# Centred output weights and regrouped output steps in a fused linear-attention and expert kernel

## The chip, the cores and the metric

One core of a Trainium2 chip runs the whole kernel in one launch. The metric is the device time in microseconds of that core, from the first to the last instruction of a launch.

## The reference

```python
x = hidden_states                                  # (2, 4096, 256)
x = x + layernorm(attn(layernorm(x)))
x = x + layernorm(ffn(layernorm(x)))

# attn: 8 heads of 32; causal, no softmax, chunks of 64, a running state
q, k, v = h @ Wq.T, h @ Wk.T, h @ Wv.T
inter  = qq @ state                                # per chunk
intra  = (qq @ kk.T * tril) @ vv
state  = state + kk.T @ vv
o = (inter + intra) / max(|sum(q * cumsum(k))|, 1)
o = rmsnorm(o) * norm_w
out = o @ Wo.T

# ffn: 8 experts, I = 256, soft routing weights w(x)
out = sum_e w_e * ((silu(h @ Wg[e]) * (h @ Wu[e])) @ Wd[e])
```

The layer norms have no weights, and eps is 1e-5.

## The kernel before

Each of the 16 blocks takes 256 rows of both batches (512 tokens, four tiles of 128). While the feed-forward part of block i-1 runs expert by expert, the attention of block i is done piece by piece between the experts' steps. An fp32 product is three products of rounded parts (high x high, low x high, high x low), so each operand has a `_hi` copy that ScalarE makes and a `_lo` remainder that VectorE makes. PE does all products in `products` (line 436).

**The order of the work** is written out by hand. `STEPS` has 28 entries; each engine walks through them in `rest` and `first_expert`. In `rest`, for expert e and half m, PE does `up(e, m)`, entry `4e-4+2m`, `down(e-1, m)`, entry `4e-3+2m`. VectorE does `hidden(e, m)` (line 1002), the first entry, `add_down(e-1, m)` (line 1024), `low_hidden(e, m)` (line 899), the second entry; ScalarE does `silu`, entry, `high`, entry. An engine does its own share of each step, in the order of its queue, and waits on semaphores for the others. GpSimd does entries 4 to 27 in a row, and of these only the carry of the state and the inverse square roots (an add and a power, lines 1193 and 1194 in `root_only`, or four instructions, lines 1184 to 1187, in `inverse_root`). The first block has its own lists, `FIRST_PE`, `FIRST_ACT`, `FIRST_DVE` and `FIRST_POOL`, with small matmuls (`warm`) between PE's steps.

**The steps the change touches**, p being a half of the block's tokens:

- `ot`: PE transposes the normalised attention output, ScalarE copies it, VectorE makes its remainder. `wo`: PE multiplies by the output weights; ScalarE copies the result from PSUM to `rows`.
- `ln2_stats`: VectorE takes bn_stats and bn_aggr of `rows` and subtracts the mean in place (line 977). `ln2_add`: x1 = rows * rstd + xs (line 985). `ln3_stats`: statistics of x1. `ln3_apply`: ScalarE normalises x1 into `rows` (line 711) with GpSimd's `rstd` and `shift`. `ft`: PE transposes it (line 591); half p waits for half p of `x1n_ready`. `ft_out`: ScalarE and VectorE make `ft_hi` and `ft_lo`, which the next block's experts read.
- `su`: VectorE adds the two chunk products of a half to the running state, eight additions on 32 partitions each (line 949).
- The PSUM tensor `att_ps` has two halves used in turn: step number n waits until step n-2 has been read out (`READ_OUT`).
- At the start, VectorE scales the rows of the output weights by `norm_w` (line 1137), ScalarE rounds them, VectorE makes the remainder, and SyncE loads the 24 expert units through eight staging buffers as these come free (`stage_free`, line 415).
- At the end, each half of the last block gets statistics, `inverse_root` on GpSimd, normalisation on ScalarE (line 711) and an addition on VectorE (line 381), and is stored.

## Time and profile before

| | us |
|---|---|
| median of 3 runs | 1494.8 (1493.81 to 1496.97) |
| the profiled execution | 1496.2, span 1494.5 |
| PE busy | 1465.5 (98%) |
| VectorE busy | 1023.8 (69%) |
| ScalarE busy | 647.2 (43%) |
| GpSimd busy | 442.9 (30%) |
| mean granted TensorE clock | 0.995 of full speed |

The span is the time from the first to the last instruction of the profiled execution, and the rest of its time lies around it. The page has the busy time of each engine, the span in 40 slices and the costliest groups of instructions. Matmuls are pipelined and their ends are modelled, so that gaps of PE are better read from start to start. Blocks 2 to 14 repeat each other to 0.1 us, with a period of 90.12 us (`ft` at 779.38 and 869.50).

### The profile page before, as it was taken

Reading aid. Unit: us, or ns where it says so; the run is one execution under the profiler, and the core shown is the slowest. Engines: PE = TensorE matmul, PEld = TensorE weight load, DVE = VectorE, ACT = ScalarE, POOL = GpSimd, SP = SyncE. Lnnn points to the kernel's source line nnn. Section 1 sums busy time; section 2 is a strip of 40 time slices with the busy share of each in tenths; the row PEclk is TensorE's granted clock in tenths of the full one; section 3 lists DMA queues with packets and bytes.
Section 4 is the critical chain, followed back from the end, with each engine's and each line's share of the span. In section 5 each row is a group of like instructions: output and inputs, shape, how many; then the busy total and the mean of one; then the engine's idle time right before and its main releaser. Section 6 shows DMA issues by size and latency. Waiting matters only on the chain. (4 is left out here: it accounts for less than half of the span.)

```text
span 1494.5 us, 37390 instructions
## 1 busy us (share of the span) xinstructions
PE 1465.5 (98%) x14438; PEld 1279.1 (86%) x14438; DVE 1023.8 (69%) x2492; ACT 647.2 (43%) x1189; POOL 442.9 (30%) x653
## 2 busy tenths in 40 slices
PE   7799999999999999999999999999999999999997
PEld 6688888888888888888888888888888888888886
DVE  6667667676776767667675776767667676776765
ACT  5443534445354443534445354443534445344333
POOL 1403414133251233414134141232413234141231
PEclk9899999999999999999999999999999999999999
DMA  5100000000000000000000000000000000000000
GB/s 171 57 2 15 15 0 14 14 14 14 0 18 10 14 14 9 19 0 14 14 14 14 0 14 14 14 14 0 28 0 14 14 14 14 0 14 16 2 8 22
DMA packets 25345, 24.59 MB, mean 16 GB/s; under 512 B 2016, under 2 KB 25056, under 8 KB 25312
## 3 DMA queue, kind: packets, MB, share of 16 engines
q1 hardware_dynamic: 25312, 24.13, 5.1%
q8 instruction: 23, 0.38, 0.1%
q14 instruction: 10, 0.08, 0.0%
HBM read 15.74 MB, written 8.39 MB: 16 GB/s over the span
## 5 line engine op out<-in xcount | busy, mean ns | idle before, releaser
L1002 DVE TENSOR_TENSOR late<-late,up_ps 128x512 f32<-128x512 f32 x256 | 174.9, 683 | 155.7 <-PE up_ps L436 99.1
L705 ACT ACTIVATE h_hi<-late 128x512 fp32r<-128x512 f32 x256 | 161.6, 631 | 247.2 <-DVE late L1002 247.2
L436 PE MATMUL down_ps<-w_hi,h_hi 128*128 128x256 f32 x976 | 264.5, 293 | 0.0
L786 ACT ACTIVATE late<-gate_ps 128x512 f32<-128x512 f32 x256 | 152.3, 595 | 252.1 <-PE gate_ps L436 252.1
L436 PE MATMUL down_ps<-w_hi,h_lo 128*128 128x256 f32 x976 | 254.1, 282 | 0.0
L1225 POOL TENSOR_TENSOR rms_in<-rms_in,minus_half 128x16 f32<-128x16 f32 x32 | 93.4, 2919 | 498.3 <-DVE rms_in L958 498.3
L899 DVE TENSOR_TENSOR h_lo<-late,h_hi 128x512 fp32r<-128x512 f32 x256 | 175.7, 686 | 65.0 <-ACT h_hi L705 65.0
L1024 DVE SCALAR_TENSOR_TENSOR late<-down_ps,route,late 128x256 f32<-128x256 f32 x364 | 158.4, 477 | 87.9 <-PE down_ps L436 84.9
L436 PE MATMUL gate_ps<-ft_hi,w_hi 128*128 128x512 f32 x512 | 204.9, 400 | 1.0 <-ACT ft_hi L705 0.8
L436 PE MATMUL gate_ps<-ft_hi,w_lo 128*128 128x512 f32 x512 | 203.5, 397 | 0.0
L436 PE MATMUL up_ps<-ft_hi,w_hi 128*128 128x512 f32 x512 | 199.7, 390 | 0.0
L436 PE MATMUL up_ps<-ft_hi,w_lo 128*128 128x512 f32 x512 | 199.7, 390 | 0.0
L436 PE MATMUL down_ps<-w_lo,h_hi 128*128 128x256 f32 x976 | 196.5, 283 | 0.0
L436 PEld LDWEIGHTS down_ps<-w_hi,h_hi 128*128 128x128 f32 x976 | 184.9, 189 | 10.4 <-issue 3.0
L436 PEld LDWEIGHTS down_ps<-w_hi,h_lo 128*128 128x128 f32 x976 | 185.9, 190 | 4.4
L436 PE MATMUL gate_ps<-ft_lo,w_hi 128*128 128x512 f32 x512 | 159.0, 392 | 0.0
L436 PE MATMUL up_ps<-ft_lo,w_hi 128*128 128x512 f32 x512 | 158.0, 390 | 0.0
L436 PEld LDWEIGHTS down_ps<-w_lo,h_hi 128*128 128x128 f32 x976 | 151.7, 191 | 0.0
L436 PEld LDWEIGHTS gate_ps<-ft_lo,w_hi 128*128 128x128 f32 x512 | 96.6, 189 | 22.0
L436 PEld LDWEIGHTS up_ps<-ft_hi,w_hi 128*128 128x128 f32 x512 | 96.4, 188 | 21.1
L436 PEld LDWEIGHTS up_ps<-ft_lo,w_hi 128*128 128x128 f32 x512 | 96.4, 188 | 20.1
L436 PEld LDWEIGHTS up_ps<-ft_hi,w_lo 128*128 128x128 f32 x512 | 96.4, 188 | 20.1
(170 smaller groups left out, 2481.9 us busy)
## 6 DMA issues: line engine op xcount, KB each, us to landing
xs<-in_x SPq DMA_DIRECT2D x32, 256.0 KB, 2.9
out_rows<-late SPq DMA_DIRECT2D x32, 256.0 KB, 2.2
late<-in_wg SPq DMA_DIRECT2D x7, 256.0 KB, 4.1
late<-in_wu SPq DMA_DIRECT2D x7, 256.0 KB, 4.4
late<-in_wd SPq DMA_DIRECT2D x6, 256.0 KB, 4.2
late<-in_wkv_t SPq DMA_DIRECT2D x1, 512.0 KB, 3.9
x<-in_wd SPq DMA_DIRECT2D x2, 256.0 KB, 4.6
late<-in_wq_t SPq DMA_DIRECT2D x1, 256.0 KB, 4.6
```

Of the source, the lines that this page charges most:

```text
L436: last = nc.tensor.matmul(dst, lhs, rhs, start=n == 0, stop=n == len(terms + low_terms) - 1)
L705: return nc.scalar.activation(dst, src, ACT.Copy)
L786: nc.scalar.activation(h_f[:, m, :], gate_ps[:, :], ACT.Silu).then_inc(silu_ready[0], 1)
L899: return nc.vector.tensor_tensor(dst, src, high_part.bitcast(f32), ALU.subtract)
L1002: nc.vector.tensor_tensor(h_f[:, m, :], h_f[:, m, :], up_ps[m][:, :], ALU.mult).then_inc(h_ready[0], 1)
L1024: last = nc.vector.scalar_tensor_tensor(dst[:, t, :], src, route[:, t, e:e + 1], acc[:, t, :], ALU.mult, ALU.add)
L1225: nc.gpsimd.tensor_tensor(rms_f[:, p, :, :], rms_in[:, p, :, :], minus_half[:, :, :], ALU.pow)\
```

## The change

1. The output weights are centred once: after scaling, VectorE subtracts from each row its mean over the outputs. `wo` then gives rows of mean zero.
2. ScalarE no longer copies the `wo` result; `ln2_stats` and `ln2_add` read it in PSUM, and the centring (line 977) is gone. The PSUM half is free again when x1 is written.
3. In `STEPS`, both halves of `ot`, of `wo` and of `ln2_stats` stand together. The second half's `ln3_apply` becomes `ln3_norm` on VectorE (with `root_only` on GpSimd), and outside the first block both halves of `ft` wait for both halves of `x1n_ready`.
4. The state addition is four scalar_tensor_tensor on 128 partitions (product times a 0/1 column plus state) in place of eight additions on 32; `state` is laid out with the chunk ahead of the batch.
5. At the start the scaling moves behind `x_norm` 1 and the remainder of the output weights behind unit 2; the load of unit 7 waits for that remainder.
6. The last half of the last block is centred, scaled and added on VectorE, with `root_only` on GpSimd.

```diff
     [("norm_apply", 0)],
-    [("ot", 0)],
+    [],
     [("norm_apply", 1), ("carry",)],
-    [("wo", 0), ("ot", 1)],
-    [("ln2_stats", 0)],
-    [("wo", 1), ("ln2_add", 0)],
-    [("ln2_stats", 1)],
-    [("ln3_stats", 0)],
-    [("ln2_add", 1), ("ln3_stats", 1)],
-    [("ln3_apply", 0)],
-    [("ln3_apply", 1)],
+    [("ot", 0), ("ot", 1)],
+    [],
+    [("wo", 0), ("wo", 1)],
+    [("ln2_stats", 0), ("ln2_stats", 1)],
+    [("ln2_add", 0)],
+    [("ln2_add", 1), ("ln3_stats", 0)],
+    [("ln3_stats", 1)],
+    [("ln3_apply", 0), ("ln3_norm", 1)],
     [("ft", 0), ("ft", 1), ("ft_out", 0), ("ft_out", 1)],
...
-FIRST_DVE = [("x_stats", 0), ("x_norm", 0), ("low", "wkv"), ("xt", 0), ("x_stats", 1), ("scale", "wo"), ("low", "wq"),
-             ("x_norm", 1), ("low", "wo"), ("xt", 1), ("unit", 0), ("su", 0), ("unit", 1), ("unit", 2), ("unit", 3), ("unit", 4),
...
+FIRST_DVE = [("x_stats", 0), ("x_norm", 0), ("low", "wkv"), ("xt", 0), ("x_stats", 1), ("low", "wq"), ("x_norm", 1),
+             ("scale", "wo"), ("xt", 1), ("unit", 0), ("su", 0), ("unit", 1), ("unit", 2), ("low", "wo"), ("unit", 3), ("unit", 4),
...
-        state = sb("state", [P, B, 5, HG, PAIR])
+        state = sb("state", [P, 5, B, HG, PAIR])
...
-            READ_OUT["wo", p] = (wo_copied, p + 1)
+            READ_OUT["wo", p] = (x1_ready, p + 1)
...
-        ATT_W = 3
+        ATT_W = 2
...
+                if u == STAGES.index(3):
+                    sp.wait_ge(wo_ready, 1)
...
-                    reach(pe, x1n_ready, a, p + 1)
+                    reach(pe, x1n_ready, a, p + 1 if is_first(a) else 2)
...
-                elif kind == "wo":
-                    p = step[1]
-                    copy(rows[:, 2 * p:2 * p + 2, :], src)\
-                        .then_inc(wo_copied[0], 1)
...
-            normalise_out(1, f)
...
-                        added = att_half(step, a)[:, i, :].rearrange("p (b g y v) -> p b g y v", b=B, g=HG, y=2)
-                        for j in range(HPG):
-                            x, y = divmod(j, 2)
-                            rows_j = slice(D * j, D * j + D)
-                            before_i, after_i = (state[rows_j, :, m, :, y * VA:(y + 1) * VA] for m in (n + i, n + i + 1))
-                            last = nc.vector.tensor_tensor(after_i, before_i, added[rows_j, :, :, y, :], ALU.add)
+                        added = att_half(step, a)[:, i, :].rearrange("p (n y v) -> p n y v", n=B * HG, y=2)
+                        for y in range(2):
+                            before_i, after_i = (state[:, m, :, :, y * VA:(y + 1) * VA]
+                                                 .rearrange("p b g v -> p (b g) v") for m in (n + i, n + i + 1))
+                            last = nc.vector.scalar_tensor_tensor(after_i, added[:, :, y, :], odd_even[:, y:y + 1], before_i,
+                                                                  ALU.mult, ALU.add)
...
                 elif kind == "ln2_stats":
                     p = step[1]
-                    reach(dve, wo_copied, a, p + 1)
-                    ln_stats(2, rows, range(2 * p, 2 * p + 2), bn2, mv2)
-                    reach(dve, moments_ready[1], a, p + 1)
+                    reach(dve, att_done, a, number_of(("wo", p), a) + 1)
+                    for b in range(B):
+                        last = nc.vector.bn_stats(bn2[:, 2 * p + b, :], att_half(("wo", p), a)[:, b, :])
+                    settle(last)
                     for t in range(2 * p, 2 * p + 2):
-                        last = nc.vector.tensor_scalar(rows[:, t, :], rows[:, t, :], mv2[:, t, 0:1], None, ALU.subtract)
-                    last.then_inc(centred[0], 1)
+                        last = nc.vector.bn_aggr(mv2[:, t, :], bn2[:, t, :])
+                    last.then_inc(moments_ready[1][0], 1)
                 elif kind == "ln2_add":
                     p = step[1]
                     reach(dve, rstd_ready[1], a, p + 1)
-                    reach(dve, centred, a, p + 1)
                     reach(dve, x1_copied, a, 0)
-                    for t in range(2 * p, 2 * p + 2):
-                        last = nc.vector.scalar_tensor_tensor(x1[:, t, :], rows[:, t, :], rstd2[:, t:t + 1], xs[:, t, :],
-                                                              ALU.mult, ALU.add)
+                    for b in range(B):
+                        t = 2 * p + b
+                        last = nc.vector.scalar_tensor_tensor(x1[:, t, :], att_half(("wo", p), a)[:, b, :], rstd2[:, t:t + 1],
+                                                              xs[:, t, :], ALU.mult, ALU.add)
                     last.then_inc(x1_ready[0], 1)
                 elif kind == "ln3_stats":
                     p = step[1]
                     reach(dve, x1_ready, a, p + 1)
                     ln_stats(3, x1, range(2 * p, 2 * p + 2), bn3, mv3)
+                elif kind == "ln3_norm":
+                    p = step[1]
+                    reach(dve, rstd_ready[2], a, p + 1)
+                    reach(dve, moments_ready[2], a, p + 1)
+                    for t in range(2 * p, 2 * p + 2):
+                        last = nc.vector.tensor_scalar(rows[:, t, :], x1[:, t, :], mv3[:, t, 0:1], rstd3[:, t:t + 1],
+                                                       ALU.subtract, ALU.mult)
+                    last.then_inc(x1n_ready[0], 1)
...
                         last = nc.vector.tensor_scalar(wo_raw[:, g, :], wo_raw[:, g, :], nw[:, g:g + 1], None, ALU.mult)
+                    settle(last)
+                    for g in range(HG):
+                        last = nc.vector.bn_stats(bn4[:, g, :], wo_raw[:, g, :])
+                    settle(last)
+                    for g in range(HG):
+                        last = nc.vector.bn_aggr(mv4[:, g, :], bn4[:, g, :])
+                    settle(last)
+                    for g in range(HG):
+                        last = nc.vector.tensor_scalar(wo_raw[:, g, :], wo_raw[:, g, :], mv4[:, g, 0:1], None, ALU.subtract)
                     last.then_inc(wo_scaled, 1)
...
             for p in range(2):
                 add_down(E - 2, p, f)
             reach(dve, out_ready, (BLOCKS - 2, 0), 2)
             for p in range(2):
                 add_down(E - 1, p, f)
                 out_stats(p, f)
-            for p in range(2):
-                out_add(nc.vector, dve, p, f)
+            dve.wait_ge(moments_ready[3][0], 2 * BLOCKS)
+            for t in range(2, 4):
+                last = nc.vector.tensor_scalar(fin[:, t, :], fin[:, t, :], mv4[:, t, 0:1], None, ALU.subtract)
+            settle(last)
+            out_add(nc.vector, dve, 0, f)
+            dve.wait_ge(x1_copied[0], BLOCKS)
+            dve.wait_ge(rstd_ready[3][0], 2 * BLOCKS)
+            for t in range(2, 4):
+                last = nc.vector.scalar_tensor_tensor(x1_kept[:, t, :], fin[:, t, :], rstd4[:, t:t + 1], x1_kept[:, t, :],
+                                                      ALU.mult, ALU.add)
+            last.then_inc(last_out_ready, 1)
...
-                    if is_first(a):
+                    if is_first(a) or p == 1:
...
-            out_root((BLOCKS - 1, 0))
+            f = (BLOCKS - 1, 0)
+            inverse_root(4, 1, slice(0, 2), f, mv4, var4, rstd4, shift4)
+            root_only(4, 1, f, mv4, var4, rstd4)
```

The two order tables below are of VectorE's loop body. First, before the change, from `hidden(5, 1)` to `low_hidden(6, 0)` (`rows` is the copied `wo` result, `xt_lo` the remainder of `ot`, `x` the tensor x1, `late` the accumulator or hidden rows):

```order
L1002 TENSOR_TENSOR late<-late,up_ps 128x512
L899 TENSOR_TENSOR xt_lo<-att_ps,xt_hi 128x512
L1024 SCALAR_TENSOR_TENSOR late<-down_ps,route,late 128x256 x2
L899 TENSOR_TENSOR h_lo<-late,h_hi 128x512
L904 BN_STATS bn<-rows 128x6 x2
L907 BN_AGGR mv<-bn 128x2 x2
L977 TENSOR_SCALAR rows<-rows,mv 128x256 x2
L283 REGISTER_ALU
L1002 TENSOR_TENSOR late<-late,up_ps 128x512
L985 SCALAR_TENSOR_TENSOR x<-rows,rstd,xs 128x256 x2
L1024 SCALAR_TENSOR_TENSOR late<-down_ps,route,late 128x256 x2
L899 TENSOR_TENSOR h_lo<-late,h_hi 128x512
```

and now, from `hidden(6, 0)` to the first `ln2_add`:

```order
L1010 TENSOR_TENSOR late<-late,up_ps 128x512
L1032 SCALAR_TENSOR_TENSOR late<-down_ps,route,late 128x256 x2
L898 TENSOR_TENSOR h_lo<-late,h_hi 128x512
L282 REGISTER_ALU
L973 BN_STATS bn<-att_ps 128x6 x2
L976 BN_AGGR mv<-bn 128x2 x2
L282 REGISTER_ALU
L973 BN_STATS bn<-att_ps 128x6 x2
L976 BN_AGGR mv<-bn 128x2 x2
L282 REGISTER_ALU
L1010 TENSOR_TENSOR late<-late,up_ps 128x512
L985 SCALAR_TENSOR_TENSOR x<-att_ps,rstd,xs 128x256 x2
```

The statistics of half 0 stood ahead of `hidden(6, 0)`; now those of both halves stand behind `low_hidden(6, 0)`, read from `att_ps`, and the subtraction is gone.

Second, the end of the same stretch; before, from `add_down(5, 1)` to `hidden(7, 1)`:

```order
L1024 SCALAR_TENSOR_TENSOR late<-down_ps,route,late 128x256 x2
L899 TENSOR_TENSOR h_lo<-late,h_hi 128x512
L985 SCALAR_TENSOR_TENSOR x<-rows,rstd,xs 128x256 x2
L904 BN_STATS bn<-x 128x6 x2
L907 BN_AGGR mv<-bn 128x2 x2
L283 REGISTER_ALU
L1002 TENSOR_TENSOR late<-late,up_ps 128x512
L1024 SCALAR_TENSOR_TENSOR late<-down_ps,route,late 128x256 x2
L899 TENSOR_TENSOR h_lo<-late,h_hi 128x512
L1002 TENSOR_TENSOR late<-late,up_ps 128x512
```

and now, from `low_hidden(6, 1)` to `hidden(7, 1)`:

```order
L898 TENSOR_TENSOR h_lo<-late,h_hi 128x512
L985 SCALAR_TENSOR_TENSOR x<-att_ps,rstd,xs 128x256 x2
L903 BN_STATS bn<-x 128x6 x2
L906 BN_AGGR mv<-bn 128x2 x2
L282 REGISTER_ALU
L1010 TENSOR_TENSOR late<-late,up_ps 128x512
L903 BN_STATS bn<-x 128x6 x2
L906 BN_AGGR mv<-bn 128x2 x2
L1032 SCALAR_TENSOR_TENSOR late<-down_ps,route,late 128x256 x2
L898 TENSOR_TENSOR h_lo<-late,h_hi 128x512
L997 TENSOR_SCALAR rows<-x,mv,rstd 128x256 x2
L1010 TENSOR_TENSOR late<-late,up_ps 128x512
```

Of x1's statistics, those of half 1 alone stood in this piece (half 0's stood just ahead of it); now both halves' do, and the normalisation of half 1 has come in ahead of `hidden(7, 1)`.

Third, VectorE at the start, from the second half's statistics of x to the first remainder of a transposed half and the unit behind it; before:

```order
L907 BN_AGGR mv<-bn 128x2 x2
L1137 TENSOR_SCALAR late<-late,nw 128x256 x2
L1139 RECIPROCAL half_inv_t<-temp 128x1
L1140 TENSOR_SCALAR half_inv_t<-half_inv_t 128x1
L899 TENSOR_TENSOR wq_lo<-late,wq_hi 128x512
L918 TENSOR_SCALAR rows<-xs,mv,rstd 128x256 x2
L899 TENSOR_TENSOR wo_lo<-late,wo_hi 128x512
L899 TENSOR_TENSOR xt_lo<-att_ps,xt_hi 128x2x256
```

and now:

```order
L906 BN_AGGR mv<-bn 128x2 x2
L898 TENSOR_TENSOR wq_lo<-late,wq_hi 128x512
L917 TENSOR_SCALAR rows<-xs,mv,rstd 128x256 x2
L1143 TENSOR_SCALAR late<-late,nw 128x256 x2
L1147 BN_STATS bn<-late 128x6 x2
L1150 BN_AGGR mv<-bn 128x2 x2
L1153 TENSOR_SCALAR late<-late,mv 128x256 x2
L1155 RECIPROCAL half_inv_t<-temp 128x1
L1156 TENSOR_SCALAR half_inv_t<-half_inv_t 128x1
L898 TENSOR_TENSOR xt_lo<-att_ps,xt_hi 128x2x256
L898 TENSOR_TENSOR w_lo<-late,w_hi 128x512
L947 SCALAR_TENSOR_TENSOR state<-att_ps,odd_even,state 128x4x33 x4
```

The remainder of the output weights (`wo_lo`) has left this stretch for a place two units on, and six instructions of centring have come in ahead of `xt_lo`.

## Rows read from the trace of the kernel before

**Rows 1.** The page, section 1: busy us (share of the span) xinstructions, each engine
```profile
PE 1465.5 (98%) x14438; PEld 1279.1 (86%) x14438; DVE 1023.8 (69%) x2492; ACT 647.2 (43%) x1189; POOL 442.9 (30%) x653
```

**Rows 2.** Waits of PE: releaser, us in total, times, longest
```profile
PE att_ps L591 <- ACT rows L711: 2.3, 13, 0.2
```

**Rows 3.** PE in order of time, one block: start us, us, engine line op
```profile
754.78 0.60 PE L578 MATMUL att_ps<-ident,shared 128*128 128x128 f32 x4
755.14 0.36 PE L436 MATMUL down_ps<-w_hi,h_hi 128*128 128x256 f32 x1
755.34 0.28 PE L436 MATMUL down_ps<-w_hi,h_lo 128*128 128x256 f32 x1
...
779.38 0.60 PE L591 MATMUL att_ps<-ident,rows 128*128 128x128 f32 x4
780.16 0.63 PE L591 MATMUL att_ps<-ident,rows 128*128 128x128 f32 x4 [0.18 <-ACT rows L711]
780.54 0.36 PE L436 MATMUL down_ps<-w_hi,h_hi 128*128 128x256 f32 x1
```

**Rows 4.** VectorE in order of time, same block
```profile
768.48 0.88 DVE L1024 SCALAR_TENSOR_TENSOR late<-down_ps,route,late 128x256 f32<-128x256 f32 x2 [0.91 <-PE down_ps L436]
...
769.87 0.74 DVE L904 BATCH_NORM_STATS2 bn<-rows 128x6 f32<-128x256 f32 x2
770.76 0.25 DVE L907 BATCH_NORM_AGGREGATE mv<-bn 128x2 f32<-128x6 f32 x2 [0.15 <-DVEq L896]
771.05 0.65 DVE L977 TENSOR_SCALAR rows<-rows,mv 128x256 f32<-128x256 f32 x2
...
776.44 0.25 DVE L907 BATCH_NORM_AGGREGATE mv<-bn 128x2 f32<-128x6 f32 x2 [0.15 <-DVEq L896]
776.75 0.69 DVE L1002 TENSOR_TENSOR late<-late,up_ps 128x512 f32<-128x512 f32 x1
...
778.14 0.69 DVE L899 TENSOR_TENSOR h_lo<-late,h_hi 128x512 fp32r<-128x512 f32 x1
```

**Rows 5.** GpSimd in order of time, same block
```profile
771.47 0.78 POOL L1194 TENSOR_TENSOR rstd<-var,minus_half 128x2 f32<-128x2 f32 x1 [0.18 <-POOLq L1179]
...
776.77 0.20 POOL L1184 TENSOR_TENSOR shift<-mv,minus_one 128x2 f32<-128x2 f32 x1 [1.11 <-DVE mv L907]
...
778.22 0.66 POOL L1187 TENSOR_TENSOR shift<-shift,rstd 128x2 f32<-128x2 f32 x1 [0.18 <-POOLq L1179]
```

**Rows 6.** PE in order of time, the start
```profile
46.40 0.35 PE L436 MATMUL att_ps<-wo_hi,xt_hi 128*128 128x256 f32 x1 [1.28 <-DVE xt_lo L899]
...
55.90 1.09 PE L591 MATMUL att_ps<-ident,rows 128*128 128x128 f32 x4 [1.30 <-DVE rows L918]
...
69.51 1.94 PE L499 MATMUL att_ps<-ident,rows 128*128 128x128 f32 x8 [2.43 <-ACT rows L711]
```

**Rows 7.** VectorE in order of time, the start
```profile
45.57 0.68 DVE L899 TENSOR_TENSOR xt_lo<-att_ps,xt_hi 128x512 fp32r<-128x512 f32 x1
...
55.02 0.73 DVE L918 TENSOR_SCALAR rows<-x,mv,rstd 128x256 f32<-128x256 f32 x2 [0.59 <-POOL rstd L1194]
```

**Rows 8.** SyncE's queue in order of time, the start
```profile
15.00 0.37 SPq L415 DMA_DIRECT2D late<-in_wu  x1
```

**Rows 9.** ScalarE in order of time, the start
```profile
26.22 0.60 ACT L705 ACTIVATE q_t<-att_ps 128x512 f32<-128x512 f32 x1 [0.89 <-PE att_ps L436]
```

**Rows 10.** The page, section 6: DMA issues, KB each, median us to landing
```profile
late<-in_wu SPq DMA_DIRECT2D x7, 256.0 KB, 4.4
```

**Rows 11.** Windows, PE alone: stretch, length, busy, granted clock, DMA share, GB/s
```profile
45.00:50.00 5.00, 3.72 (x33) 1.00 0.10 33
70.00:75.00 5.00, 5.00 (x22) 0.71 0.00 2
```

**Rows 12.** VectorE in order of time, the end
```profile
1487.65 0.25 DVE L907 BATCH_NORM_AGGREGATE mv<-bn 128x2 f32<-128x6 f32 x2
...
1490.89 0.69 DVE L381 TENSOR_TENSOR late<-late,shared 128x512 f32<-128x512 f32 x1 [1.28 <-ACT shared L711]
```

More of the change, by code:

```diff
@@ L442, in with_state @@
                     last = nc.tensor.matmul(dst[C * g:C * g + C, i, c:c + PAIR], q_t[half, g, tok:tok + C],
-                                            state[half, b, 2 * p + i, g, :], start=b == 0 and x == i, stop=b == B - 1 and x != i)
+                                            state[half, 2 * p + i, b, g, :], start=b == 0 and x == i, stop=b == B - 1 and x != i)
                 return last
@@ L723, in att_step @@
                 kind = step[0]
[L724 removed]
+                if step in PSUM_STEPS and kind not in ("s", "su", "wo", "ft"):
                     reach(act, att_done, a, number_of(step, a) + 1)
```

39 lines of the change are left out of this document (19 added, 20 removed).

## The prediction

> **What bounds the kernel now.** I read the page first: PE is busy 98% of the span, every other engine under 70% [rows 1]. So only two things can change the time: what PE has to do, and the places where it stands still. The change gives PE the same matmuls. The waits of PE, read next, name one stall that repeats: 13 times, the second half of `ft` waits for ScalarE's `ln3_apply` [rows 2]. The list puts it at 0.2 us, because matmul ends are modelled. PE's order of time shows it from start to start: four transposes of `ot` take 0.36 us (754.78 to 755.14), but the two halves of `ft` begin 0.78 us apart (779.38, 780.16), so the stall is 0.42 us [rows 3]. Then comes VectorE's order of time in the same stretch: from 768.48, where it has waited 0.91 us for PE, it goes without a pause to the `low_hidden` at 778.14 [rows 4]. That run of work, not VectorE's 69%, is what the change must be held against, for it moves work of VectorE into this run. The rest of the time lies in the start (about 70 us with gaps) and the last 5 us.
>
> **The loop: the regrouped steps.** PE first. The first matmul behind a group of transposes takes 0.36 us instead of 0.28 [rows 3]; joining both `ot` leaves one such place fewer per block, -0.08 us. So `down(5, 0)`, whose end VectorE awaits at 768.48, comes at 768.40, and `ft` could start at 779.30.
>
> Now VectorE from 768.40, with PE, ScalarE and GpSimd on time. An instruction starts about 0.09 us before the one ahead of it ends. Between `add_down(5, 0)` and `low_hidden(7, 0)` lay 9.66 us (768.48 to 778.14) [rows 4]. Into this run come:
> - one more `ln2_stats`, for half 0 did its own before 768: 0.89 us from bn_stats to bn_aggr (769.87 to 770.76), and 0.28 to what follows, by the 0.29 to 0.31 seen behind other bn_aggr (770.76 to 771.05, 776.44 to 776.75): +1.17 [rows 4].
> - half 0's `ln2_add`. A pair of scalar_tensor_tensor on 256 columns takes 0.88 us, less the overlap [rows 4]: +0.80.
> Out of it go the centring, 0.65 less 0.09 [rows 4], and about 0.11 us of wait, because an addition no longer stands right ahead of the statistics of its own result: -0.67.
>
> Sum: 9.66 + 1.17 + 0.80 - 0.67 = 10.96. `low_hidden(7, 0)` starts at 779.36, and the next instruction at 779.96. That is `ln3_norm` of half 1. Its `rstd`: its bn_aggr (0.25 us) and `add_down(6, 0)` (0.88) stand ahead of `low_hidden(7, 0)`, so with the overlaps it starts at 778.41 and its moments are out at 778.66; `root_only` takes 0.20 and 0.18 us and the power's 0.78 [rows 5], so it is there by about 779.9, just in time. Half 0's `inverse_root` takes 1.65 us (776.77 to 778.22, and 0.20 unhindered) [rows 5] from some 776.9, and ScalarE then has over a microsecond for its half. Not it, but VectorE, is late. `ln3_norm` takes 0.73 us, and PE starts its transposes 0.15 us behind it (55.02, 55.90) [rows 6, 7]: 779.96 + 0.73 + 0.15 gives about **780.87**. Both halves wait for this, so the stall is 780.87 - 779.30 = 1.57 us, where 0.42 stood. Per block: +1.15 - 0.08 = **+1.07 us**. It recurs in each of the 15 blocks, as PE's gap gives VectorE no lead: the next run again begins with PE's `down(5, 0)`. I count all alike, though blocks 1 and 15 stalled less: 15 x 1.07, less a little for those, is **+15.8 us**.
>
> The bounds. Below: if the three pauses behind a bn_aggr (0.31 us to the next start, where 0.25 less the overlap would be 0.16) vanish and each group is 0.02 tighter, the stall is 1.0 and the block costs +0.5. Above: an operation of GpSimd that meets `low_hidden` on VectorE was held: 0.66 us at 778.22 instead of 0.20 [rows 5]. The power now falls across `low_hidden(7, 0)`. If it is held, `ln3_norm` starts at 780.3, +0.4. Not held is likelier, since the power begins a quarter microsecond before. With a small late wait at `down(6, 0)`, which needs `low_hidden(6, 1)` nearly at once, the top is +1.7 a block.
>
> **Reading PSUM.** Four bn_stats and four additions of a block now read PSUM. A product of 512 columns with one source in PSUM took 0.69 us (776.75), a difference with both in SBUF 0.69 (778.14) [rows 4]: I price the change of source at nothing. The Trainium skill, VectorE: DVE Perf Modes, section "The TRN2 errata", gives a VectorE operation 120 fixed cycles from PSUM and 58 from SBUF; by that the eight would cost 0.5 us more a block and the sum would be 8 us higher. The equal rows speak against it.
>
> **ScalarE and the state addition.** Two copies of 512 columns a block leave ScalarE, and `ln3_apply` of half 1. None bounded PE but the last. The state additions, four for eight, make VectorE idle earlier in the block, where PE does not wait for it: nothing. If the wider form were twice as long each, it would be even; ahead of 768 VectorE has slack in any case. The centred weights cost nothing in the loop, and without them the copy and centring could not go.
>
> **The start.** In the first block VectorE bounds. The remainder of `ot` 1 stood at 45.57, behind half 0's statistics and centring, which waited for ScalarE's copy [rows 7]; PE's `wo` 1 followed at 46.40 after a gap of 1.28 us [rows 6]. Now statistics start a microsecond earlier and the remainder is bound by `ot` 1 itself: about -1.1 us. Half 1's copy and centring would save another 1.2 us, but GpSimd's two roots in a row take most of it: -0.3. So `ft` and all behind it: **-1.4 us**. Against it stands the queue of SyncE: unit 7's load left at 15.00 [rows 8]; now it waits for `wo_lo`. That follows `xt_lo` 1 (at 17, as before), three units and a state addition of 1.2 us or less, 0.6 us for each of the others: about 21.4, and all later loads stand behind it. ScalarE wants units 7 and 8, two copies of 0.6 us, and then has 0.89 us to spare before the `q` 1 copy at 26.22 [rows 9], so it wants unit 7 at 24.2. The queue is empty by then, so I take under 3 us to landing and no cost; with the median of 4.4 us [rows 10] two units would come late and `q` 1 by up to 1.5 us, and so the start. Bounds -2 to +0.5.
>
> **The end.** The last half's moments are out at 1487.90 (1487.65 and 0.25), and its addition began only at 1490.89, 1.28 us after the first half's had ended at 1489.61 [rows 12]; it took 0.69. Now the subtraction hides behind the wait for half 0, whose addition runs as before; `rstd` is out at about 1489.1 by the `root_only` time above; then two scalar_tensor_tensor, 0.88 us, go from 1489.52 to 1490.40, where 1491.58 stood. The two stores then lie closer: **-1.15 us** (bounds -0.8 to -1.2).
>
> **Sum.** +15.8 - 1.4 - 1.15 = +13.2 us. Of the profiled execution's 1496.2 this makes 1509.4; it is 1.4 above the median of 1494.8, on which I forecast: **1508.0 us**.
>
> **Rivals.**
> 1. *VectorE keeps up, and the kernel is faster* (0.10). `ln3_norm` would have to start 1.6 us earlier, by 778.4. For: copies, centring and four state additions are gone, and half of the final normalisation runs beside the other. Then the stall of 0.42 and the 0.08 go: 15 x -0.5 - 2.5 = -10, 1484.8. Against: nothing in the rows leaves 1.6 us out of an unbroken run of 11. It decides at a stall under 0.3 us.
> 2. *The gains and a smaller stall cancel* (0.05): a stall of about 0.7, 1494.8 within 3.
> 3. *The clock falls in the stall* (0.06). At the start PE's clock fell after a gap of 2.43 us: at 70 to 75 it was granted 0.71 on average, part of it at 1.2 GHz; with the gap of 1.28 us it stayed at 2.4 GHz [rows 6, 11]. A stall of 1.6 us lies between, and nearer the harmless one. If each stall cost what those 5 us lost, 0.29 x 5 = 1.5 us, another 15 x 1.5 come on top: 1530.
> 4. *Reads of PSUM are dearer, or GpSimd is held* (0.10 together, in my range). Held: 15 x 0.4 = 6 more. Dearer by what a bn_stats lacks to a scalar_tensor_tensor (pairs of 0.74 and 0.88, so 0.07 each) [rows 4]: 15 x 8 x 0.07 = 8 more. About 1515.
> 5. *The change does not do what it says*: the order tables show the moved rows; nothing is left for it.
>
> **How the numbers follow.** The stall longer than before at the price of about 1.57: 0.69, 1500 to 1519; rival 4 adds 0.10 in it; rival 3 beyond it 0.06; rivals 1 and 2 below 0.15. The range of **1499 to 1520** holds about eight in ten. A measurement of this kernel tells 0.2%, 3 us, from no change: faster 0.10, same 0.05, slower 0.85.
>
> **What would show it.** Right: both halves of `ft` begin at one time, 0.72 us of transposes behind a gap, with VectorE's `ln3_norm` as releaser in PE's waits, 15 times, about 1.3 us in the list; the period of a block 91.2 us instead of 90.12; VectorE without idle from `add_down(5, 0)` to `ln3_norm`; the last store 1.2 us nearer to PE's end. Wrong: a stall under 0.5, another releaser (GpSimd's `rstd`, ScalarE's half), idle time of VectorE inside that run, bn_stats from `att_ps` well over 0.41 us each, or a clock under 1.00 in the loop.

## The result, and the profile after

The changed kernel takes **1510.68 us** (median of 4 runs, 1506.99 to 1511.68), the kernel before 1495.39 (4 runs beside it). The ratio is 1.0098, with a 95% interval of 1.0077 to 1.0118: 15.3 us slower, where 1508.0 in a range of 1499 to 1520 was forecast. The profiled execution took 1510.73 us with a span of 1509.0. TensorE was granted 0.95 of its clock through that profile's loop, where the profile before had 1.00. The other three runs, at a mean of 0.993 to 0.998, took 1506.99 to 1511.68 us, so the lower clock does not show in the total; what it is worth in a block stands in the section on why.

The page of the kernel after, section 1 (busy us, share of the span, instructions), answers to [rows 1]:

```profile
PE 1466.6 (97%) x14438; PEld 1280.0 (85%) x14438; DVE 981.9 (65%) x2339; ACT 615.0 (41%) x1125; POOL 416.5 (28%) x621
```

VectorE does 42 us less, ScalarE 32 and GpSimd 26 less, and the kernel is slower. PE does what it did. PE's list of waits (releaser, us in total, times, longest) tells where the time went; it answers to [rows 2]:

```profile
PE att_ps L595 <- DVE rows L997: 18.0, 17, 1.3
...
PE att_ps L544 <- issue: 2.3, 1, 2.3
```

ScalarE's 13 waits are gone. In their place `ft` waits for VectorE's `ln3_norm` (L997), 15 times in the loop at about 1.06 us, and twice in the start. PE in order of time, block 8 (start us, us, engine line op, idle before and its releaser), beside [rows 3]:

```profile
786.57 0.61 PE L440 MATMUL up_ps<-ft_lo,w_hi 128*128 128x512 f32 x2
788.24 1.08 PE L595 MATMUL att_ps<-ident,rows 128*128 128x128 f32 x8 [1.06 <-DVE rows L997]
789.07 0.37 PE L440 MATMUL down_ps<-w_hi,h_hi 128*128 128x256 f32 x1
```

Both halves are one group of eight transposes now. In the kernel before, the line that ends `up` stands ahead of the `ft` at 779.38 [rows 3]:

```profile
778.93 0.62 PE L436 MATMUL up_ps<-ft_lo,w_hi 128*128 128x512 f32 x2
```

`ft` follows it 0.45 us after it begins, so PE was free here at 787.02, and the stall is 1.22 us. VectorE in the same block, beside [rows 4]:

```profile
776.12 0.88 DVE L1032 SCALAR_TENSOR_TENSOR late<-down_ps,route,late 128x256 f32<-128x256 f32 x2 [3.50 <-PE down_ps L440]
...
777.51 0.76 DVE L973 BATCH_NORM_STATS2 bn<-att_ps 128x6 f32<-128x256 f32 x2
778.42 0.25 DVE L976 BATCH_NORM_AGGREGATE mv<-bn 128x2 f32<-128x6 f32 x2 [0.15 <-DVEq L895]
778.58 0.74 DVE L973 BATCH_NORM_STATS2 bn<-att_ps 128x6 f32<-128x256 f32 x2
779.47 0.25 DVE L976 BATCH_NORM_AGGREGATE mv<-bn 128x2 f32<-128x6 f32 x2 [0.15 <-DVEq L895]
779.68 0.69 DVE L1010 TENSOR_TENSOR late<-late,up_ps 128x512 f32<-128x512 f32 x1
780.29 0.87 DVE L985 SCALAR_TENSOR_TENSOR x<-att_ps,rstd,xs 128x256 f32<-128x256 f32 x2
...
786.76 0.69 DVE L898 TENSOR_TENSOR h_lo<-late,h_hi 128x512 fp32r<-128x512 f32 x1
787.36 0.74 DVE L997 TENSOR_SCALAR rows<-x,mv,rstd 128x256 f32<-128x256 f32 x2
```

The reader is to see three things: 3.50 us of idle time right ahead of `add_down(5, 0)`, no pause but those behind a bn_stats from there to `ln3_norm`, and both halves' statistics inside that stretch. Before, half 0's statistics lay ahead of it.

The start and the end. PE's first `ft`s, SyncE's load of unit 7, and VectorE's last instructions, beside [rows 6], [rows 8] and [rows 12]:

```profile
57.05 0.63 PE L595 MATMUL att_ps<-ident,rows 128*128 128x128 f32 x4 [1.07 <-DVE rows L997]
58.97 0.63 PE L595 MATMUL att_ps<-ident,rows 128*128 128x128 f32 x4 [1.29 <-DVE rows L997]
```
```profile
22.53 0.37 SPq L419 DMA_DIRECT2D late<-in_wu  x1
```
```profile
1503.35 0.25 DVE L906 BATCH_NORM_AGGREGATE mv<-bn 128x2 f32<-128x6 f32 x2
1503.63 0.65 DVE L1191 TENSOR_SCALAR shared<-shared,mv 128x256 f32<-128x256 f32 x2
1504.62 0.69 DVE L380 TENSOR_TENSOR late<-late,shared 128x512 f32<-128x512 f32 x1 [0.34 <-ACT shared L715]
1505.23 0.87 DVE L1197 SCALAR_TENSOR_TENSOR late<-shared,rstd,late 128x256 f32<-128x256 f32 x2
```

`ft` 1 of the start is 3.1 us later (58.97 for 55.90), not 1.4 earlier. From the last bn_aggr to the last addition's end it is 2.75 us (1503.35 to 1506.10), where it was 3.93 (1487.65 to 1491.58).

**The account.** PE's last matmul moved from 1484.79 to 1500.50, by 15.7 us; the span by 14.5, so the end gave 1.2. Of the 15.7, 1.67 were there at block 1's `ft` (148.93, then 150.60), 1.05 of it its own wait; 14.05 came between there and block 15's `ft` (1410.20, then 1425.92). One block takes 91.10 us (blocks 2 to 15, 241.67 to 1425.92 over 13) where it took 90.12.

### The profile page after: what moved, and what is told of

Its sections match the earlier page's. It is cut to its first block and busy times, and to the rows that moved or that the text cites. A ratio compares the mean times of both kernels' runs of the same rounds, so it can differ in the third digit from the quotient of the medians.

```text
span 1509.0 us, 37144 instructions
## 1 busy us (share of the span) xinstructions
PE 1466.6 (97%) x14438; PEld 1280.0 (85%) x14438; DVE 981.9 (65%) x2339; ACT 615.0 (41%) x1125; POOL 416.5 (28%) x621
```

## The experiments

Each was run beside the kernel before, and the ratios are to it. "Block" is the mean distance of `ft` from one block to the next, blocks 2 to 15, in the run's profile.

### 1. Both halves' statistics moved into VectorE's wait

```
-    [("wo", 0), ("wo", 1)],
-    [("ln2_stats", 0), ("ln2_stats", 1)],
+    [("wo", 0), ("wo", 1), ("ln2_stats", 0), ("ln2_stats", 1)],
+    [],
```

> The changed kernel with one move on VectorE: both halves' ln2_stats (2.17 us of its order, 777.51 to 779.68 in block 8) go ahead of add_down(5, 0), into the 3.50 us in which VectorE waits for down(5, 0); the wo products end about 774.9 there. PE's order is untouched. My theory (VectorE's unbroken run from add_down(5, 0) to ln3_norm is too long by the moved work): the stall at ft, 1.22 us (788.24 against the 787.02 at which PE was free), goes, and with it most of the 0.11 us that eight transposes take more behind a pause: 15 x 1.3 = 20 us less than the change, about 1491, period of a block 89.75. Rival 'the joint wait of ft, or ln3_norm on VectorE, is at fault': the moved statistics help little, over 1505. Rival 'reads of PSUM cost more': the run of VectorE would still be shortened, so as theory one, but the statistics would show more than 0.76 us a pair. Rival 'the clock or the start': no change, 1510.

Measured: 1501.11 us, ratio 1.0031 (1.0021 to 1.0042), block 90.23. Two thirds of the loss went, so the moved work is its cause; but not all of it, and less than I expected. VectorE and then PE, block 8 of this kernel, in order of time:

```profile
776.19 0.69 DVE L1010 TENSOR_TENSOR late<-late,up_ps 128x512 f32<-128x512 f32 x1 [1.35 <-PE up_ps L440]
...
783.88 0.73 DVE L997 TENSOR_SCALAR rows<-x,mv,rstd 128x256 f32<-128x256 f32 x2
```
```profile
783.82 0.61 PE L440 MATMUL up_ps<-ft_lo,w_hi 128*128 128x512 f32 x2
784.75 1.06 PE L595 MATMUL att_ps<-ident,rows 128*128 128x128 f32 x8 [0.32 <-DVE rows L997]
```

With 2.17 us less to do, VectorE came so early to `hidden(6, 1)` that it waited there for PE. A lead ends at the next instruction that reads PE's output: the unbroken run now begins at 776.19, and from there to `ln3_norm` are 7.69 us, ending 0.48 too late (784.75 for 784.27).

### 2. Half 0's statistics alone, a smaller dose

```
-    [("wo", 0), ("wo", 1)],
-    [("ln2_stats", 0), ("ln2_stats", 1)],
+    [("wo", 0), ("wo", 1), ("ln2_stats", 0)],
+    [("ln2_stats", 1)],
```

> As the first, but half 0's statistics alone go into VectorE's wait (half 1's stay behind add_down(5, 0) and low_hidden(6, 0)): a smaller dose, 1.07 us (777.51 to 778.58). Theory: the stall at ft shrinks from 1.22 to about 0.15 us, each block by about 1.1 us: 15 x 1.1 = 16.5 less, about 1494. Rivals: over 1505, as for the first.

Measured: 1499.88 us, ratio 1.0022 (1.0013 to 1.0031), block 90.23: half the dose, the same block. PE and VectorE, block 8:

```profile
786.19 1.06 PE L595 MATMUL att_ps<-ident,rows 128*128 128x128 f32 x8 [0.31 <-DVE rows L997]
```
```profile
777.63 0.69 DVE L1010 TENSOR_TENSOR late<-late,up_ps 128x512 f32<-128x512 f32 x1 [0.27 <-PE up_ps L440]
...
785.32 0.73 DVE L997 TENSOR_SCALAR rows<-x,mv,rstd 128x256 f32<-128x256 f32 x2
```

Again 7.69 us from `hidden(6, 1)`. So of the 1.07 us moved, 0.27 were already of no use, and the other 1.10 of experiment 1 as well. My 1494 for this one rested on the same mistake.

### 3. Each half of `ft` waits for its own half

```
-                    reach(pe, x1n_ready, a, p + 1 if is_first(a) else 2)
...
+                        reach(pe, (x1n_act, x1n_dve)[p], a, 1)
...
-    shift3, rstd3).then_inc(x1n_ready[0], 1)
+    shift3, rstd3).then_inc(x1n_act[0], 1)
```

> The changed kernel, but each half of ft waits for its own half of the rows (two semaphores, one for ScalarE's half, one for VectorE's). VectorE's and every other order is untouched. Theory: half 0 may start when ScalarE is done with it, at about 787.3 instead of 788.24, and half 1 still waits for ln3_norm: what is gained is half 0's transposes, 0.36 to 0.45 us a block, 15 x 0.4 = 6, about 1504.5, and half 1 still starts behind a wait for VectorE. Rival 'the joint wait is the cause': the whole 1.22 us goes, under 1495.

Measured: 1505.26 us, ratio 1.0055 (1.0042 to 1.0068), block 90.48. The joint wait costs 0.5 to 0.6 us a block, the transposes of half 0 that could have been done meanwhile; the stall itself is not its doing. In this profile `ft` still begins 0.35 us after PE is free in block 8 (786.74 for 786.39), now behind ScalarE's half. It came as expected.

### 4. The output steps at their old places, the rest as changed

```
-    [],
+    [("ot", 0)],
     [("norm_apply", 1), ("carry",)],
-    [("ot", 0), ("ot", 1)],
-    [],
-    [("wo", 0), ("wo", 1)],
-    [("ln2_stats", 0), ("ln2_stats", 1)],
-    [("ln2_add", 0)],
-    [("ln2_add", 1), ("ln3_stats", 0)],
-    [("ln3_stats", 1)],
-    [("ln3_apply", 0), ("ln3_norm", 1)],
+    [("wo", 0), ("ot", 1)],
+    [("ln2_stats", 0), ("ln2_add", 0)],
+    [("wo", 1)],
+    [("ln2_stats", 1)],
+    [("ln3_stats", 0)],
+    [("ln2_add", 1), ("ln3_stats", 1)],
+    [("ln3_apply", 0)],
+    [("ln3_norm", 1)],
```

> The changed kernel with the places of the output steps as before the change (ot, wo and the statistics of half 0 ahead of those of half 1), but for ln2_add 0, which comes right behind ln2_stats 0, since wo 1 now takes the PSUM half that ln2_add 0 reads; ln3_norm 1 stays on VectorE, behind low_hidden(7, 0). Centred weights, reads of PSUM, state additions and the end are the change's. Theory (the regrouping alone costs, the rest saves): VectorE's run from add_down(5, 0) is shorter than before the change by half 0's addition's absence and the centring, 9.66 - 0.65, so ln3_norm is out by 779, ahead of PE: no stall at ft, 0.42 us a block less than before, -6.3, the end -1.2, the start +0.4: about 1488.5. Rival 'the PSUM reads or ln3_norm on VectorE are at fault': slower than before, 1500 or more.

Measured: 1531.89 us, ratio 1.024 (1.0227 to 1.0253). `ft` never waits in the loop, as theory had it, but another wait of PE took its place. PE's waits of this kernel, then GpSimd, VectorE and PE in order of time:

```profile
PE att_ps L440 <- DVE x L985: 30.4, 16, 2.0
```
```profile
783.48 0.70 POOL L1221 TENSOR_TENSOR rstd<-var,minus_half 128x2 f32<-128x2 f32 x1 [0.18 <-POOLq L1206]
```
```profile
784.21 0.88 DVE L985 SCALAR_TENSOR_TENSOR x<-att_ps,rstd,xs 128x256 f32<-128x256 f32 x2 [1.18 <-POOL rstd L1221]
```
```profile
785.14 0.38 PE L440 MATMUL att_ps<-wo_hi,xt_hi 128*128 128x256 f32 x1 [1.96 <-DVE x L985]
```

With `ot` 1 between them, `wo` 1 writes the PSUM half of `wo` 0, and that is free only when `ln2_add` 0 has read it, behind statistics and GpSimd's root. Before the change a copy of ScalarE freed it. So the reads from PSUM and the grouping of the output steps are not two independent edits: in the old order the reads from PSUM cost more than the grouping does. That only this grouping avoids it is not shown. I had left out that wait.

### 5. The additions moved too

Half 0's addition (in `stats_add_early`, atop experiment 1), then half 1's too (`all_early_stages`, `all_early`). The table of the last against the change:

```
-    [("wo", 0), ("wo", 1)],
-    [("ln2_stats", 0), ("ln2_stats", 1)],
-    [("ln2_add", 0)],
-    [("ln2_add", 1), ("ln3_stats", 0)],
+    [("wo", 0), ("wo", 1), ("ln2_stats", 0), ("ln2_stats", 1)],
+    [("ln2_add", 0)],
+    [("ln2_add", 1)],
+    [("ln3_stats", 0)],
```

> As stats_both_early, and half 0's ln2_add moved ahead too, from behind hidden(6, 1) to behind low_hidden(6, 0). In stats_both_early VectorE stood idle 1.35 us ahead of hidden(6, 1) (776.19) and from there ran without a pause to ln3_norm, so the run now begins at hidden(6, 1), which waits for PE's up(6, 1), and still ends 0.48 us late (ft at 784.75, PE free at 784.27). Theory (the length of the unbroken run from VectorE's last wait for PE decides): the pair of additions, 0.79 us, fits into the 1.35 us, the run is shorter by it, the stall of 0.48 goes: 15 x 0.48 = 7 us under stats_both_early, about 1494, period 89.7; faster than before the change by some 2 us. Rival 'ft is bound by something else by then, ScalarE's half or GpSimd's roots': 1499 to 1501, another releaser at ft.

Measured: 1499.72 us, ratio 1.0029 (1.0014 to 1.0044), block 90.19. Against experiment 1's 1.0031 nearly nothing is gained; the same mistake a third time, though the trace of experiment 1 could have told it. VectorE of this kernel, block 8:

```profile
774.60 0.69 DVE L1010 TENSOR_TENSOR late<-late,up_ps 128x512 f32<-128x512 f32 x1 [0.56 <-PE up_ps L440]
775.97 0.87 DVE L1032 SCALAR_TENSOR_TENSOR late<-down_ps,route,late 128x256 f32<-128x256 f32 x2 [0.68 <-PE down_ps L440]
...
782.25 0.73 DVE L997 TENSOR_SCALAR rows<-x,mv,rstd 128x256 f32<-128x256 f32 x2
```

The run now begins at `add_down(5, 1)`, which waits for `down(5, 1)`: 6.28 us, and `ft` comes at 783.12 where PE was free at 782.69. Read that way, what has to move is half 1's addition, into the 0.68 us:

> early_and_stages with one more move: half 1's ln2_add from behind low_hidden(6, 1) to behind hidden(6, 1), ahead of add_down(5, 1). In stats_add_early VectorE waited 0.68 us for down(5, 1) (775.97) and from there ran without a pause to ln3_norm, 0.43 us too late for PE; so the last wait for PE had only gone on to the next instruction that reads PE's output. Theory (what counts is the work between the last wait for PE and ln3_norm): with the addition in that wait (hidden(6, 1) 774.60, the pair 775.20, add_down(5, 1) still at 775.98) ln3_norm starts at 781.47, the rows are out at 782.35 and PE is free at 782.69: no stall at ft, 15 x 0.43 = 6.5 us under early_and_stages, about 1491, period of a block 89.7; 4.7 us faster than before the change. Rival 'ScalarE's half or GpSimd's roots are next': a releaser of that kind at ft and 1493 to 1497. Rival 'the moved addition delays down(6, 1) on PE': a wait at down with h_lo as releaser.

Measured: 1491.23 us, ratio 0.9969 (0.9958 to 0.998), block 89.75. **Faster than both kernels**, by 0.3% than the one before, and where it was expected. The staging table is part of it, so the last run took that back:

> all_early_stages with the change's own table of staging buffers back: the three moves of VectorE's steps alone. before_late_load showed that the pause in s 1 and its fall of the clock (ft 1 of the start 3.1 us later) are there with the late loads alone, but that block 1's ft was late by 0.16 us only, since the later fall of the clock at 70 to 75 us stayed away. Theory (what the start loses by the late loads is given back by 150 us): within a microsecond of all_early_stages, 1490.5 to 1492.5. Rival (the 2.2 us by which stages was under the change are a real gain of the spread loads): about 1493.5, and early_and_stages lay 2.4 us under stats_add_early in the same way.

Measured: 1491.87 us, ratio 0.9978 (0.9968 to 0.9988), block 89.76. VectorE and PE in its block 8:

```profile
772.68 0.69 DVE L1010 TENSOR_TENSOR late<-late,up_ps 128x512 f32<-128x512 f32 x1 [0.26 <-PE up_ps L440]
...
775.70 0.73 DVE L997 TENSOR_SCALAR rows<-x,mv,rstd 128x256 f32<-128x256 f32 x2
```
```profile
776.14 0.62 PE L440 MATMUL up_ps<-ft_lo,w_hi 128*128 128x512 f32 x2
776.59 1.05 PE L595 MATMUL att_ps<-ident,rows 128*128 128x128 f32 x8
```

No wait is left at `ft`: it begins 0.45 us after the line before it. The rows of `ln3_norm` are out, by the 0.88 us from its start to `ft` in the change, at 776.58, so there is no slack either.

| kernel | last wait of VectorE for PE | to `ln3_norm`, us | stall at `ft`, us | block, us |
|---|---|---|---|---|
| the change | `add_down(5, 0)` | 11.24 | 1.22 | 91.10 |
| half 0's statistics early | `hidden(6, 1)` | 7.69 | 0.47 | 90.23 |
| both | `hidden(6, 1)` | 7.69 | 0.48 | 90.23 |
| and `ln2_add` 0 | `add_down(5, 1)` | 6.28 | 0.43 | 90.19 |
| and `ln2_add` 1 | `hidden(7, 0)` | 3.02 | none | 89.76 |

### 6. The start: late loads

In the first block's attention `s` is PE's step that multiplies keys by queries, `o` the one that multiplies the result by the values; the number is the half. The first trial spreads the loads in the changed kernel by another table of staging buffers.

```
-        STAGES = [4, 5, 6, 7, 1, 2, 0, 3] * 2 + [4, 5, 0, 1, 2, 3, 4, 5]
+        STAGES = [4, 5, 6, 7, 1, 2, 0] + [4, 5, 3, 6, 7, 1, 2, 0, 3] + [4, 5, 0, 1, 2, 3, 4, 5]
```

> The changed kernel with another table of staging buffers for the 24 weight blocks of the start: unit 7 goes into buffer 4 (free when unit 0 is converted, about 18.5) and buffer 3, which holds the output weights until wo_lo is there, is used first by unit 9. In the changed kernel unit 7's load left at 22.53 and nine loads followed within 4 us; DMA was over its full share at 25 to 30 us, and in s 1 PE stood 2.35 us (2.9 and 3.2 in two other profiles) with nothing that it waited for in the profile, then ran at a granted clock down to 0.6. Before the change the loads were spread from 15.00 on, the pause was 0.65 and the clock stayed. Theory (the burst of loads holds up PE's instructions, and the pause lets the clock fall): the loads are spread again, the pause goes back under 1.2 us, no fall of the clock at 30 to 40 us, ft 1 of the start at 55 to 57 us instead of 59 to 61, total 2.5 to 4 us under the change: about 1507. Rival 'chance, or the changed order of the engines in the start': the pause of over 2 us stays, same time as the change.

Measured: 1508.47 us, ratio 1.009 (1.0073 to 1.0106); the change's is 1.0098 (1.0077 to 1.0118), so in time the two are not told apart. In the profile the pause in `s` 1 fell to 0.43 us, but one of 1.41 came a step later, in `o` 1, and the clock of the stretch from 35 to 40 was 0.70 all the same. Inconclusive. The same table with experiment 5's first additions:

> stats_add_early and stages together. If both theories hold their gains add: about 1494 - 3 = 1491, faster than before the change by 5 us. If stages does nothing: 1494. If neither: 1500.

Measured: 1497.36 us, ratio 1.0013 (1.0003 to 1.0022), beside 1.0029 (1.0014 to 1.0044) without the table: the intervals overlap here too. Experiment 5 has a third such pair, 0.9969 with the table and 0.9978 without. Each pair is too close to decide, but all three lie the same way, by 0.8, 1.6 and 0.9 parts in a thousand, so a gain of 1 to 2 us by spread loads is not ruled out. The clean test is the other way round, the late load alone in the kernel before:

```
-                    sp.wait_ge(w_ready, stage_free(u))
+                    sp.wait_ge(w_ready, ATT_W + 3 if u == 7 else stage_free(u))
```

> The kernel before with one number changed: the start's load of unit 7 waits until unit 2 is converted (about 22 us, where it left at 15.00), and all later loads stand behind it, as in the change. Nothing else differs: the output weights, the orders of the engines and the loop are those of before. Theory (the late burst of loads holds up PE's instructions in s 1 and lets the clock fall): the pause in s 1 grows from 0.65 us to 2 or more, the granted clock falls between 30 and 40 us, ft 1 of the start comes at 58 to 60 us instead of 55.9, total 2 to 4 us more, about 1498.5. Rival 'the changed orders or the longer preparation of the output weights cost it': no change, 1495.6.

Measured: 1496.24 us, ratio 1.001 (1.0001 to 1.0019). SyncE, then PE in order of time, of this kernel:

```profile
22.37 0.37 SPq L415 DMA_DIRECT2D late<-in_wu  x1
```
```profile
30.05 0.38 PE L540 MATMUL att_ps<-q_t,kz 64*64 64x64 f32 x9
33.02 1.77 PE L540 MATMUL att_ps<-q_t,kz 64*64 64x64 f32 x55 [2.59 <-issue]
...
59.00 0.63 PE L591 MATMUL att_ps<-ident,rows 128*128 128x128 f32 x4 [1.30 <-DVE rows L918]
...
149.09 1.03 PE L591 MATMUL att_ps<-ident,rows 128*128 128x128 f32 x8
```

The late load alone gives the start of the change: the pause in `s` 1 (2.59 us, 2.35 in the change, 0.65 before), slower matmuls behind it (55 in 1.77 us; 1.04 before), `ft` 1 at 59.00 (58.97 in the change). That `ft` 1 agrees to 0.03 us is in part chance: the change's profile was already 0.83 us later at `s` 0 (24.53, here 23.70). And yet block 1's `ft` comes at 149.09, 0.16 us after that of before. The windows (stretch, length, busy of PE, PEld, DVE, ACT, POOL, granted clock, DMA share, GB/s) tell where it came back, this kernel first, then the kernel before:

```profile
30.00:35.00 5.00, 2.41 (x67) 2.16 (x66) 1.65 (x5) 3.57 (x7) 2.90 (x1) 0.76 0.62 202
...
55.00:60.00 5.00, 1.88 (x14) 1.27 (x12) 3.68 (x11) 0.94 (x2) 1.80 (x3) 0.99 0.32 105
...
70.00:75.00 5.00, 3.75 (x21) 3.26 (x22) 2.58 (x4) 3.68 (x8) 3.67 (x9) 1.00 0.00 2
```
```profile
30.00:35.00 5.00, 3.97 (x151) 3.52 (x145) 4.30 (x9) 3.16 (x6) 2.91 (x1) 1.00 0.22 72
...
55.00:60.00 5.00, 3.32 (x9) 2.55 (x10) 3.68 (x7) 0.83 (x2) 0.00 (x0) 0.58 0.00 1
```

The kernel before runs 30 to 35 at full clock, but 55 to 60 at 0.58 and 70 to 75 at 0.71 [rows 11]; with the late load it is the other way round. Of the 3.10 us lost by `ft` 1, 1.74 are left at block 1's first transposes (71.25 for 69.51 [rows 6]) and 0.16 at its `ft`. `all_early`, with late loads and a pause of 3.17 us, is the same: `ft` 1 at 59.60, clock 1.00 from 60 to 75, block 1's `ft` at 148.34. But it does not always come back. Of the eight profiles of this document with late loads, these two and the change's have no fall between 65 and 75 us; the other five have one, to between 0.66 and 0.84, and their block 1's `ft` is at 151.7 to 154.6, where the six with earlier loads have 148.5 to 151.9 (stalls of up to 1.2 us at `ft` and 2 at `wo` 1 of `old_steps` are in these). So the profiles in which the late load costs next to nothing look like the good case, not the rule; how much it costs on average is not shown.

### 7. The end and the state additions, each alone in the kernel before

```
-            for p in range(2):
-                out_add(nc.vector, dve, p, f)
...
+            for t in range(2, 4):
+                last = nc.vector.tensor_scalar(fin[:, t, :], fin[:, t, :], mv4[:, t, 0:1], None, ALU.subtract)
+            settle(last)
+            out_add(nc.vector, dve, 0, f)
...
+            for t in range(2, 4):
+                last = nc.vector.scalar_tensor_tensor(x1_kept[:, t, :], fin[:, t, :], rstd4[:, t:t + 1], x1_kept[:, t, :],
+                                                      ALU.mult, ALU.add)
```

> The kernel before, with only the end of the last block as in the change: the last half's subtraction hidden behind the wait, root_only, two scalar_tensor_tensor on VectorE. My term of the sum was -1.15 us, read at the distance from PE's last matmul to the end of the span, 9.71 before (1484.79 to 1494.5) and about 8.5 after; in the total 1.1 us less, at the edge of what can be measured. Rival: nothing, if the stores bound the end (0).

Measured: 1494.42 us, ratio 0.9994 (0.9985 to 1.0003). In time alone it is nothing that can be told; in the profile PE's last matmuls start at 1484.17 and the span is 1492.7, 8.5 us later, where it was 9.7: 1.2 us, the same as in the change.

```
-                        for j in range(HPG):
-                            x, y = divmod(j, 2)
-                            rows_j = slice(D * j, D * j + D)
...
+                        for y in range(2):
...
+                            last = nc.vector.scalar_tensor_tensor(after_i, added[:, :, y, :], odd_even[:, y:y + 1], before_i,
+                                                                  ALU.mult, ALU.add)
```

> The kernel before with the masked state additions alone (four scalar_tensor_tensor on all partitions for eight additions on 64, and the state's dimensions swapped). I priced them at nothing in the time: VectorE has slack there. Expected: within 0.2% of before, VectorE's work of a step 1.38 us where it was 2.53. Rival: the swapped dimensions or the idle brought forward change PE's places: a period other than 90.12.

Measured: 1494.10 us, ratio 0.9986 (0.9975 to 0.9997): within 0.2% by its middle, perhaps a little faster. VectorE's group in the list of lines (busy us, mean ns), before and with the edit:

```profile
L949 DVE TENSOR_TENSOR state<-state,att_ps 32x132 f32<-32x132 f32 x256 | 73.6, 288 | 7.9 <-DVEq L896 2.1
```
```profile
L948 DVE SCALAR_TENSOR_TENSOR state<-att_ps,odd_even,state 128x132 f32<-128x132 f32 x128 | 39.5, 350 | 8.4 <-PE att_ps L569 3.1 <-DVEq L896 2.0
```

34 us of VectorE's work gone, and by the median 1.8 us of time: nearly all of that work lay where VectorE had slack. But the rival, a period other than 90.12, came true in small: a block takes 90.04 us (90.01 to 90.03, and 90.36 for the last), which makes 0.7 of the 1.8 us from block 1's `ft` to block 15's. The only difference of size in VectorE's run is the step from the last bn_aggr of x1 to `hidden(7, 0)`, which the edit does not touch:

```profile
778.14 0.25 DVE L907 BATCH_NORM_AGGREGATE mv<-bn 128x2 f32<-128x6 f32 x2 [0.15 <-DVEq L896]
778.35 0.69 DVE L1002 TENSOR_TENSOR late<-late,up_ps 128x512 f32<-128x512 f32 x1
```

It is 0.21 us, where the kernel before has 0.31 (776.44, 776.75 [rows 4]). Why stays open.

Its profile also has something that speaks against a simple story of the start. PE in order of time:

```profile
29.16 0.60 PE L569 MATMUL att_ps<-v_sb,k_sb 64*64 64x66 f32 x11 [2.67 <-issue]
```

The loads leave as before the change (unit 7's at 14.84), and a long pause is there all the same, in another step, with the clock at 0.50 from 30 to 35 us.

## Why the prediction was right, point by point

**The loop, +15.8: right in mechanism and place, a little large a block.** The stall has the releaser, the count and the shape foretold, and moving the work out of the run took it away. In size: from `add_down(5, 0)` to `ft` I had 12.47 us and it was 12.12. Of this 0.35, 0.03 is a slip of mine: 779.96 + 0.73 + 0.15 is 780.84, not 780.87. From the end of the chain backwards, the steps of 0.60 and 0.88 were met; the rest lies in the pauses behind a bn_aggr, priced at 0.28 to 0.31 to the next start and measured at 0.16 and 0.21 (778.42 to 778.58, 779.47 to 779.68). The bound below had this. One of these pauses is as short with the state additions alone (experiment 7). So the stall was 1.22, not 1.57; against it the eight transposes in one group took 0.83 us (788.24 to 789.07), where I had 0.72. That makes 1.22 - 0.42 + 0.83 - 0.74 - 0.08 = +0.81 a block (0.74 is the 0.36 and 0.38 of [rows 3]). The profile of the change shows +0.98; the one of `stages`, whose loop is the same, +0.84 (90.96). The difference goes with the granted clock, 0.95 in the one and 1.00 in the other. The windows of a block, the change and then `stages`:

```profile
697.00:788.00 91.00, 90.01 (x893) 78.56 (x893) 60.03 (x144) 37.51 (x69) 25.86 (x38) 0.95 0.04 12
```
```profile
697.00:788.00 91.00, 89.93 (x893) 78.49 (x893) 59.81 (x144) 37.53 (x70) 25.93 (x38) 1.00 0.04 12
```

So 15 blocks made some 13 us at the higher clock, 15 at the lower. That the profile's loop comes so near to +15.8 is partly luck: by the higher clock the term was about 3 us too large. And since the change's runs at the higher clock took as long as the profiled one, some 2 us of their time are not placed; no profile of them is there.

**The state additions, at nothing:** nearly. Alone they took 0.7 us out of the loop (90.04 us a block for 90.12), by a pause of VectorE that they do not touch.

**GpSimd held:** no. The second half's root took 0.69 us, at 786.54, beside VectorE's `low_hidden(7, 0)`. VectorE, not `rstd`, was last, as said.

**Reading PSUM, at nothing: right.** Statistics from PSUM took 0.76 and 0.74 us a pair, from SBUF 0.74 [rows 4]; the addition with its source in PSUM 0.87, and that of the last half, all in SBUF, 0.87 (1505.23). The rule of the Trainium skill (VectorE: DVE Perf Modes, section "The TRN2 errata", 120 fixed cycles from PSUM for 58 from SBUF) would, as an estimate, have made the sum 8 us higher; these rows do not agree with it for these shapes.

**The start, -1.4: wrong.** Two steps of it failed. "So I take under 3 us to landing and no cost" looked only at ScalarE's wait for units 7 and 8, and there it held; but the load and the seven queued behind it left within 3.5 us (22.53 to 26.01) and PE stood still in `s` 1, waiting for nothing that the profile shows, then ran at the lower clock. Experiment 6 shows this with the late load alone; `before_state` shows that such a pause also comes without it. And "the remainder of `ot` 1 ... about -1.1" missed that `wo` 1 also waits for the PSUM half that `ln2_add` 0 reads: 1.1 us in PE's list, the same rule that experiment 4 ran into. From `ot` 1 to `wo` 1 it is 3.03 us (46.75, 49.78), where it was 3.25 (43.15, 46.40): 0.2 gained, not 1.1. The other step, -0.3 between `wo` 1 and `ft` 1, was met (9.19 us for 9.50). In the change's profile what the start loses by 59 us is mostly back by 150, +0.45 at block 1's `ft` (1.67 less the stall of 1.22), but that is one of the better three of eight; the late load alone has a ratio of 1.001 (1.0001 to 1.0019). The start's share in the median stays open within some 2 us.

**The end, -1.15:** 1.2, in two kernels.

**The rivals.** VectorE keeps up: it does so only with three more moves that the change did not make, and then the kernel is faster, by less than the 10 us I gave (3.7). A clock that falls in the stall: no. The profile did have a clock under 1.00 in the loop, which I had named as a sign of being wrong, but it was level at 0.95, and `stages` has the same stalls at 1.00. My argument for this rival was incomplete all the same: I took a pause of 1.28 us for harmless, while in the kernel before the clock was 0.58 from 55 to 60 us, behind pauses of 1.45 and 1.30.

The sum in the profile was 13.2 foretold, 14.5 measured (span to span): loop +15.3 (14.05 and block 1's 1.22) for +15.8, start +0.45 for -1.4, end -1.2 for -1.15. Two errors of opposite sign partly met.

## What to carry to other kernels

Where one engine bounds a kernel, the work that may be added to a second engine is what fits between its last wait for the first and the result the first needs; its busy share over the span (65% here) did not tell it. Ahead of that wait there is room for free, and each lead won there is lost again at the next instruction that waits for the bounding engine. So when work is moved, mark every such wait in the stretch and give to each window only what it holds: the same instructions cost 15 us in one order and, with the statistics and additions of `ln2` some microseconds earlier, gained 3.7.

And who reads a PSUM tile directly instead of copying it out holds it until the last reader is through; see first which step is to write it next.
